# Cross-attention: the engine that issues the small transfers of the negated maxima

## What is computed

```python
q = (x @ Wq).reshape(b, n, 32, 16)
k, v = jnp.split(ctx @ Wkv, 2, axis=-1)      # reshaped alike
q = apply_axial_rope(q, pos_map); k = apply_axial_rope(k, ctx_pos_map)
logits = jnp.einsum('bqhd,bkhd->bhqk', q, k) * 16 ** -0.5
w = jax.nn.softmax(logits, axis=-1)
attn = jnp.einsum('bhqk,bkhd->bqhd', w, v).reshape(b, n, 512)
return attn @ Wout + bout
```

## Time and profile before

| | |
|---|---|
| median of 3 runs | 1539.27 us (1538.8 to 1540.97) |
| the profiled execution | 1543.37 us, its span 1541.6 us |
| TensorE busy in the span | 1350.0 us, 88% |
| TensorE's weight loads | 1085.7 us, 70% |
| VectorE | 881.5 us, 57% |
| ScalarE | 469.6 us, 30% |
| GpSimd | 510.4 us, 33% |
| `b_qT<-b_mT`, SP | 128 transfers, 4.0 KB |
| L1110, exponentials | 128, mean 1116 ns, 142.8 us |

### The profile page before, as it was taken

One profiled execution on the slowest core, in us unless ns is written; L12 is line 12 of the kernel. 1 busy time (PEld: TensorE's weight loads), 2 busy tenths in 40 slices (PEclk: granted clock), 3 DMA queues, 4 the chain that ended last, 5 costly groups with the idle time before them and its releaser, 6 DMA issues. The chain is left out here.

```text
span 1541.6 us, 24041 instructions
## 1 busy us (share of the span) xinstructions
PE 1350.0 (88%) x8442; PEld 1085.7 (70%) x8442; DVE 881.5 (57%) x1532; ACT 469.6 (30%) x731; POOL 510.4 (33%) x348
## 2 busy tenths in 40 slices
PE   5899999992579999999846899999999999999960
PEld 4677777771556777677535788888878799999950
DVE  5566666664578788777656456555575422222224
ACT  3222222222236566666622211111111132223210
POOL 1122221211644334343023016351160463664035
PEclk9999999996879999999977899999999999999985
DMA  7000000002265555555149103230000343443146
GB/s 293 1 1 1 0 0 0 0 1 78 100 185 170 149 152 153 153 152 166 45 168 393 43 21 130 97 133 21 21 34 14 130 138 129 141 153 125 66 137 225
DMA packets 90939, 158.78 MB, mean 103 GB/s; under 512 B 8176, under 2 KB 59504, under 8 KB 88560
## 3 DMA queue, kind: packets, MB, share of 16 engines
q1 hardware_dynamic: 84592, 123.14, 24.9%
q0 software_dynamic: 6272, 34.61, 6.2%
HBM read 88.25 MB, written 68.94 MB: 102 GB/s over the span
## 5 line engine op out<-in xcount | busy, mean ns | idle before, releaser
L1576 DVE SCALAR_TENSOR_TENSOR residual<-c_yp,c_shared,residual 128x512 f32<-128x512 f32 x176 | 127.4, 745 | 143.4 <-PE c_yp L43 137.4
L968 DVE TENSOR_REDUCE b_mx<-b_rt 128x4 f32<-128x1024 f32 x128 | 156.3, 1221 | 59.1 <-PE b_rt L793 59.0
L1110 ACT ACTIVATE b_pf<-b_rt,b_zero 128x1024 f32<-128x1024 f32 x128 | 142.8, 1116 | 120.9 <-PE b_rt L805 120.7
L41 PE MATMUL c_fc<-c_xh,c_w 128*128 128x512 f32 x352 | 137.1, 390 | 0.0
L43 PE MATMUL c_fc<-c_xh,c_w 128*128 128x512 f32 x352 | 137.0, 389 | 0.0
L42 PE MATMUL c_fc<-c_xl,c_w 128*128 128x512 f32 x352 | 137.0, 389 | 0.0
L41 PE MATMUL c_fc<-c_ring,c_xTl 128*128 x312 | 105.8, 339 | 4.7 <-DVE c_xTl L1581 4.7
L1590 DVE TENSOR_TENSOR c_hTl<-c_eh,c_hTh 128x384 fp32r<-128x384 f32 x39 | 21.7, 558 | 144.9 <-ACT c_hTh L1700 134.6
L43 PE MATMUL c_fc<-c_ring,c_xTh 128*128 x312 | 101.3, 325 | 0.0
L42 PE MATMUL c_fc<-c_ring,c_xTh 128*128 x312 | 101.3, 325 | 0.0
L1676 ACT ACTIVATE c_s<-c_fc 128x512 f32<-128x512 f32 x44 | 26.3, 598 | 239.6 <-PE c_fc L43 239.6
(11 more groups left out here) (288 smaller groups left out, 3457.6 us busy)
## 6 DMA issues: line engine op xcount, KB each, us to landing
c_eraw<-in_c_we POOLq DMA_DIRECT2D x8, 2176.0 KB, 9.8
b_pack<-b_hi SPq DMA_DIRECT2D x64, 256.0 KB, 2.4
b_qT<-b_pack SPq DMA_DIRECT2D x64, 200.0 KB
b_kT<-b_pack SPq DMA_DIRECT2D x64, 192.0 KB
c_xe<-c_rows_in SPq DMA_DIRECT2D x39, 256.0 KB, 2.9
c_rows_out<-c_ye SPq DMA_DIRECT2D x39, 256.0 KB, 2.0
c_rows_in<-c_xe SPq DMA_DIRECT2D x19, 512.0 KB
c_rows_out<-c_xe SPq DMA_DIRECT2D x19, 512.0 KB
```

Source lines behind the costliest of these rows:

```text
L41: nc.tensor.matmul(out, ll, rh, start=start, stop=False)
L968: nc.vector.tensor_reduce(out=mx[:, :, 2 * p:2 * p + 2].rearrange("p t e -> p e t"), in_=rt[:, 0:2, :].rearrange("p e (t s) -> p e t s", s ...
L1110: nc.scalar.activation(pf[:, s:s + 2, :], rt[:, 2:4, :], ACT.Exp, scale=XD ** -0.5, bias=zero[:, :]).then_inc(e_done, 1)
L1576: nc.vector.scalar_tensor_tensor(out=X[:, t, :], in0=yp[:, (n * 4 + k) % 3, :], scalar=shared[:, t:t + 1], in1=X[:, t, :], op0=ALU.mult, o ...
```

## The change

The function `maxima` goes from SP to ScalarE as `maxima_move`, with the same wait, the same four transfers, the same semaphore, and one step earlier: step 4k+4, at the end of that step's program, behind ScalarE's `maxima_out` of the same step. The wait is on `mt_done`, which ScalarE's own copy raises. (`values_out` stands between in the program, but falls on odd steps only.)

```diff
--- before.py
+++ after.py
@@ -754,19 +754,8 @@
                         sp.dma_start(as_f32(packed[64 * e:64 * e + n, 4 * f:4 * f + 4, :]), pack_dram[g, which, 0:n, at, c, :])\
                             .then_inc(chunk_in[f], 16)
 
-            def maxima(g, k):
-                sp.wait_ge(mt_done, g * 4 + (k + 1))
-                for c in range(2):
-                    for e in range(2):
-                        row = 64 * e + 48 + c
-                        sp.dma_start(as_f32(qT[row:row + 1, 4 * k:4 * k + 4, :]),
-                                     as_f32(mT[8 * c + e:8 * c + e + 7:2, k % 2, :])).then_inc(m_moved[k % 2], 16)
-
             def body(b, live):
                 for i in range(T):
-                    for k in range(4):
-                        for d in due(i, live, 4 * k + 5):
-                            maxima(b + d, k)
                     for d in due(i, live, -14):
                         if not (isinstance(b, int) and b + d + 1 >= B):
                             context(b + (d + 1))
@@ -1098,6 +1087,14 @@
                     act.wait_ge(m_moved[k % 2], g * 128 + k // 2 * 64)
                 nc.scalar.copy(mT[:, k % 2, :], av[0:32, S:2 * S]).then_inc(mt_done, 1)
 
+            def maxima_move(g, k):
+                act.wait_ge(mt_done, g * 4 + (k + 1))
+                for c in range(2):
+                    for e in range(2):
+                        row = 64 * e + 48 + c
+                        act.dma_start(as_f32(qT[row:row + 1, 4 * k:4 * k + 4, :]),
+                                      as_f32(mT[8 * c + e:8 * c + e + 7:2, k % 2, :])).then_inc(m_moved[k % 2], 16)
+
             def values_out(g, q):
                 act.wait_ge(av_done, g * 8 + (q + 3))
                 nc.scalar.copy(at[:, q % 2, :], av[:, 0:S]).then_inc(at_done, 1)
@@ -1138,6 +1135,9 @@
                             maxima_out(b + d, k)
                     for d, q in quads(i, live, LAGV):
                         values_out(b + d, q)
+                    for k in range(4):
+                        for d in due(i, live, 4 * k + 4):
+                            maxima_move(b + d, k)
 
             act.wait_ge(presets, 2)
             bodies(act, body)
```

## The result

| | before | after |
|---|---|---|
| median | 1540.12 us | 1580.71 us |
| ratio | | 1.0256 (1.0229 to 1.0283) |
| the profiled execution | 1543.37 us, span 1541.6 | 1581.49 us, span 1579.7 |
| first instruction behind cross-attention (VectorE, statistics of the next part) | 790.64 us | 830.52 us |
| one group in the steady part, copy k = 2 to copy k = 2 | 43.7 us | 47.8 us |

The change costs 40.6 us, where 30.9 were forecast. All of it is in cross-attention: its end moves by 39.9 us, and what follows it takes 1.8 us less in this execution.

What follows compares the result with a forecast made beforehand. TensorE's in-order stream was taken to bound cross-attention. Delays of 1.9 + 2.6 + 8.8 + 9.2 in the steady part and 8.4 in filling and draining sum to 30.9 us, on 1539.27 giving 1570.2 us; range 1542 to 1585.

Steps and rivals of the forecast that it cites:

- The mechanism: Cross-attention: four issues and the wait hold ScalarE 2.49 us per copy; only what exceeds the step's slack delays TensorE.
- the forecast's own case: ScalarE's issue costs 0.5 to 0.7 us per transfer: +17.7 to +41 us, 1557 to 1580 us; chance 0.70.
- a dearer issue: Rival: ScalarE's issue costs toward 0.9 us per transfer, up to 1606 us; chance 0.08.
- The term of the steady steps: Cross-attention, groups 1 to 6, 24 copies: TensorE late by what the 2.49 us hold leaves above slack, 21.05 us.
- The first copy: Filling part, first of the 32 copies: 7.8 us of room, so it costs nothing.
- Draining: Group 7, from its first copy to the end of cross-attention: 1.92, 2.89 and 0.81 us by the slack working.
- The rival of the falling clock: Rival: the clock falls in TensorE's new gaps, or late hi copies reach the chunks; 1585 us and up; chance 0.05.
- The gain on SP: SP gives up 80 us of issuing, but TensorE waits on none of the transfers behind it: gain nothing.
- The wait: ScalarE's wait for its own copy, ahead of the four transfers: 0.03 us each.
- What follows cross-attention: Stages before and behind cross-attention were to stay unchanged.
- a short issue: Rival: ScalarE issues faster than SP; at 0.29 us each +3.5 us, 1542.8; under 0.2 us nothing, 1539.3; chance 0.13.
- SP as the hidden limit: Rival: TensorE's idle weight loads before `rows` wait behind SP's queue; freeing SP returns up to 12.7 us, 1527; chance 0.04.

Runs made afterwards that it cites:

- e7_first: Kernel before, but ScalarE issues only the very first of the 32 groups of maxima, SP all others: 1547.17 us, ratio 1.0036.
- after_again: The changed kernel, unaltered, run once more in a later set beside its own kernel before: 1582.68 us, ratio 1.0269.
- e6_ends: Changed kernel, but ScalarE issues only the 12 groups of the filling and draining parts, SP those in the loop: +18.6 us, ratio 1.0127.
- e3b_hold_long: Kernel before, SP issuing, plus on ScalarE the wait and a dummy copy of 2910 columns in place of the transfers: 1576.40 us against 1541.74, ratio 1.0234.
- e10_merged_sp: Kernel before with two merged transfers of 8 KB issued by SP instead of four of 4 KB: 1541.18 us, ratio 0.9995.
- e4_wait: Kernel before, SP issuing, with only the wait for its own copy added on ScalarE: 1522.02 us, ratio 1.0007.
- e2_spread: Changed kernel, but ScalarE issues each group's four transfers in small portions spread over steps 4k+4 to 4k+6: 1524.37 us, ratio 1.0027.

## Why the prediction was right, and where its sum was short

- **The mechanism, right.** ScalarE's issue of a transfer is as dear as SP's (581 for 573 ns), and only what exceeds the step's slack reaches TensorE. The four slacks read from the earlier trace rows were 0.96 to 2.18 us; measured they are 0.98 to 2.09, none off by more than 0.11. In the k = 0 steps the wait that ends last is that of the k gemm for xl (1.66 us), which the prediction put beside its own path through the maximum and `rows` as "about as late".
- **The total inside the range, in part by luck.** 1580.7 us lies at the upper edge of the forecast's own case (1557 to 1580), whose edges stood for issues of 0.5 and 0.7 us, though the issue measured 0.58. The range reached beyond that for a dearer issue, and what filled it was something else: the first copy, the clock and the time behind the last issue.
- **The term of the steady steps, 21.05 us, measured 23.86.** The hold was mis-sized: 2.49 us taken, mostly 2.57 us measured ahead of an exponential and 2.71 to 2.98 us ahead of the copies of xh and v in groups 2 to 6. The transfers themselves were right (2.41 to 2.56 for four, and once 2.79; 2.46 taken). What was left out is the time from the last issue to the start of the next instruction.
- **The first copy, 0 us, measured 3.80.** This step of the prediction failed: "the first copy has 7.8 us of room" counted to the next exponential, but behind it in ScalarE's order stand the two copies of xh, on which I had let the k = 0 steps of all the other groups hang. I applied the right rule to six copies and the short one to the seventh. The first use of the queue adds 0.6 us, and TensorE at its lower clock makes the following work longer. Alone this hold makes its step 2.9 to 3.5 us longer (e7_first).
- **Draining, 5.62 us from the first copy of group 7 on, measured 8.70** (3.48 + 2.80 + 2.42); 8.16 in after_again, 8.69 in e6_ends, 8.20 in e3b_hold_long. The rival of the falling clock was named at a chance of 0.05 and dismissed by a stretch that was busy for 7.97 of 10 us, in which no gap of TensorE was longer than 0.73 us. Here the clock fell behind a gap of 1.64 us. The matmuls at the lower level are 1.6 us of the difference in the first step, if the working of the hold (1.92) is right. The 1.6 us of the last step can't be put down to the change: they come in three kernels without a transfer of ScalarE there, and stay away in after_again and e6_ends, which have them.
- **The gain on SP, 0**: right (e10_merged_sp).
- **The wait, 0.03 us**: right (e4_wait, and 0.03 us between the copy's end and the first transfer in the timelines).
- **What follows cross-attention**, predicted unchanged, is 1.8 us shorter in the profiled execution; its granted clock differs there too, and the spread between executions is of that size.
- The rivals: a short issue is ruled out by 581 ns; the Trainium skill's some 50 ns for a sequencer's dispatch ("DMA: Bandwidth & Descriptors", anatomy of one DMA), which would have made the change free, describes the GpSimd path and doesn't hold for ScalarE here. An issue above 0.9 us occurs at the first use (1195 ns), and once more in after_again (1107 ns, at 468.29 us). SP as the hidden limit is ruled out by e10. The prediction's argument that the idle pieces ahead of TensorE's weight loads were all of 0.36 to 0.41 us doesn't fit, whose longest is 1.0 us; the verdict rests on e10 and not on it.

## What to carry to other kernels

An engine that is idle for 40% of a stretch can still have no room: ask for its slack between two of its instructions that sit in a loop with the bottleneck, and compare the whole held time with that, with every instruction that stands behind the new one in its order, not only the next in its loop. One of these transfers of 4 or 8 KB costs its issuing engine about 0.6 us, so merge such transfers first, and put each behind a long instruction whose result it doesn't need instead of behind the one whose result it does. And price the filling and draining steps singly: in the profiled execution groups 0 and 7 carried 16 of the 40 us for 8 of 32 holds.

## What the runs showed of the hardware that I had not expected

- ScalarE's first four transfers take 3.03 to 3.04 us to issue instead of 2.42, at 440, 510 or 742 us alike.
- A transfer that needs no result in flight is issued beside the running instruction ahead of it (577.64 beside 577.63 in e2_spread, and so for 96 of its 128).
- In the draining part one gap of TensorE of 1.64 us is followed by a granted clock of 0.68 and 0.50 over 8 us; a gap of nearly the same length in the steady part, the 1.66 us ahead of 632.71 us, left it at 1.00. In the last step the same gap of 1.06 us is followed by a fall in one execution and not in another. So the gap's length alone doesn't decide it; what does isn't settled.
